# A state-space block with an FP4 FFN on one core: kept blocks in HBM, a lag of 20 steps, and the norms' squares on ScalarE

## The reference

```python
# first part, per sequence
x_proj, z = split(x @ W_in)                      # 256 -> 2 x 512
x_conv = silu(causal_conv4(x_proj) + conv_b)     # along the tokens
ssm = x_conv @ W_xproj                           # 33 columns: delta, B (16), C (16)
delta = softplus(ssm[..., 0])
h_mean = einsum(x_conv, delta * B) / L           # a sum over the WHOLE sequence
y = (h_mean x C + D * x_conv) * silu(z)
x = layernorm(x + y @ W_out)
# second part, per token: FP4 rounding in blocks of 16 before each product
h = silu(fp4(x) @ fp4(w_gate)) * (fp4(x) @ fp4(w_up))   # 256 -> 704
x = layernorm(x + fp4(h) @ fp4(w_down))
```

## Time and profile before

| | |
|---|---|
| three runs | 2200.66, 2203.39, 2206.25 us |
| the profiled execution | 2204.03 us, its span 2202.1 us |
| PE, PEld | 1990.6 us (90%), 1583.8 (72%) |
| DVE | 1756.7 us (80%) |
| ACT, POOL | 1111.5 (50%), 1115.6 (51%) |
| granted PE clock, mean | 0.98 |
| DMA | 90.53 MB, queue share 12.2% |
| chain that ended last | PE 76%, issue 5%, DVE 4%, ACT 3% |

### The profile page before, as it was taken

One profiled execution on the slowest core, in us unless ns is written; L12 is line 12 of the kernel. 1 busy time (PEld: TensorE's weight loads), 2 busy tenths in 40 slices (PEclk: granted clock), 3 DMA queues, 4 the chain that ended last, 5 costly groups with the idle time before them and its releaser, 6 DMA issues.

```text
span 2202.1 us, 37847 instructions
## 1 busy us (share of the span) xinstructions
PE 1990.6 (90%) x10532; PEld 1583.8 (72%) x10532; DVE 1756.7 (80%) x3548; ACT 1111.5 (50%) x2100; POOL 1115.6 (51%) x1643
## 2 busy tenths in 40 slices
PE   1887899899999999899999999899999999877776
PEld 1655688688877888688877888688876888666665
DVE  6234788798978888789877888798887888788875
ACT  2665455555545555455544556455544555423332
POOL 2223455466545556455644555465554556445543
PEclk9999999999999999999999999999999999999998
DMA  2111111111111111111111111111111111000000
GB/s 79 50 56 43 34 49 44 44 43 45 49 41 34 44 48 45 36 49 49 41 38 41 44 44 48 38 49 44 39 41 39 49 45 35 29 20 25 20 20 15
DMA packets 77089, 90.53 MB, mean 41 GB/s; under 512 B 8881, under 2 KB 59953, under 8 KB 76849
## 3 DMA queue, kind: packets, MB, share of 16 engines
q1 hardware_dynamic: 76848, 87.73, 12.2%
HBM read 37.37 MB, written 16.78 MB: 25 GB/s over the span
## 4 chain that ended last, share of the span: by engine, by line
PE 76%; issue 5%; DVE 4%; ACT 3%; POOL 1%; ACTq 0%; DVEq 0%; POOLq 0%
PE pgu L489 23%; PE pd L489 14%; PE pd L537 9%; PE pa L489 6%; PE pb L489 6%; PE pc L571 4%; PE pc L519 4%; PE pe_ L631 2%; PE pa L559 2%; PE pc L496 2%; PE pe_ L548 1%; PE pd L638 1%; DVE hbuf L990 1%; DVE qsh L820 1%; PE pa L615 1%
## 5 line engine op out<-in xcount | busy, mean ns | idle before, releaser
L489 PE MATMUL pgu<-wgu_hi,xqT 128*128 128x512 f32 (+1 forms) x1536 | 427.7, 387 | 0.9 <-issue 0.9
L489 PE MATMUL pd<-wd_hi,hqT 128*128 128x256 f32 (+1 forms) x1536 | 334.5, 299 | 18.7 <-DVE r L1012 15.5
L489 PEld LDWEIGHTS pgu<-wgu_hi,xqT 128*128 128x128 f32 x1536 | 279.8, 190 | 75.8 <-issue 27.6
L537 PE MATMUL pd<-wout,g 128*128 128x256 f32 x1024 | 259.9, 398 | 49.6 <-DVE hqT L980 35.2
L489 PEld LDWEIGHTS pd<-wd_hi,hqT 128*128 128x128 f32 (+1 forms) x1536 | 255.8, 190 | 57.4 <-issue 23.8
L946 DVE SCALAR_TENSOR_TENSOR acc<-xps,cw,acc 128x512 f32<-128x512 f32 x256 | 248.7, 972 | 24.4 <-POOL acc L429 23.7
L418 POOL TENSOR_SCALAR rs<-mv 128x1 f32<-128x1 f32 x128 | 61.6, 481 | 396.4 <-DVE mv L1027 228.8
L537 PEld LDWEIGHTS pd<-wout,g 128*128 128x128 f32 x1024 | 191.5, 195 | 79.7 <-issue 56.0
L741 ACT ACTIVATE hqT<-pe_ 128x512 fp32r<-128x512 f32 x128 | 76.2, 595 | 335.3 <-PE pe_ L631 335.3
L402 POOL TENSOR_TENSOR xv<-xnq,qsx 128x256 f32<-128x256 bf16 x128 | 79.5, 621 | 300.1 <-DVE xnq L839 300.1
L489 PE MATMUL pgu<-wgu_lo,xqT 128*128 128x512 f32 (+1 forms) x768 | 228.3, 379 | 0.0
(11 more groups left out here) (132 smaller groups left out, 4669.2 us busy)
## 6 DMA issues: line engine op xcount, KB each, us to landing
xcr<-xcs SPq DMA_DIRECT2D x128, 256.0 KB, 2.3
xin<-in_L_attn_x_dram SPq DMA_DIRECT2D x32, 512.0 KB, 3.9
xres<-in_L_attn_x_dram SPq DMA_DIRECT2D x128, 128.0 KB, 2.1
out_dram<-outb SPq DMA_DIRECT2D x128, 128.0 KB, 1.7
szr<-in_L_attn_W_in_dram SPq DMA_DIRECT2D x1, 1024.0 KB, 7.4
szr<-in_L_ffn_w_down_dram SPq DMA_DIRECT2D x1, 704.0 KB, 8.6
szr<-in_L_ffn_w_gate_dram SPq DMA_DIRECT2D x1, 640.0 KB, 4.5
szr<-in_L_ffn_w_up_dram SPq DMA_DIRECT2D x1, 640.0 KB, 5.7
```

Of the source, the lines that this page charges most:

```text
L489: mm = pe.matmul(bank, lhsT, rhs, start=(m == 0), stop=(m == len(pairs) - 1))
L537: mm = pe.matmul(pd[:, 0:DM], g[:, (s + 1) % 2, c, j * P:(j + 1) * P], wout[:, c, :], start=(c == 0), stop=(c == NB - 1))
```

## The change

- `szr` and `xcr` go. Silu(z) and the convolved block are written to two HBM tensors and read back into `xl` and `zl`, two slots each, one step ahead. The weights' scratch space moves.
- The second half runs 20 steps behind (`LAG` = 5 supersteps) instead of 16, so there is no late y; the state's division by L (`hcat`) stands at the end of the fourth step of the next sequence's first superstep. `walk` unrolls eight supersteps, then loops over sequences 2 to 7.
- The norms: DVE's two adds now also put out their sum (`accum_out`), ACT squares the deviations with an output of their sum (`deviations`), POOL works from these. The four statistics operations on DVE go.
- The order of every engine's step is written anew. The transposes of h put their last two blocks into `pb` instead of `pd`; the last norm's add comes at the start of the next step; C's transposes move from j = 1 to j = 3. h's two rounding steps stay the last DVE operations of their step, and h's product with the scales the last of POOL's.

```diff
+    LAG = SPS + 1
...
+    xc_hbm = nc.dram_tensor("xc_hbm", [NT, P, ST], F32)
+    sz_hbm = nc.dram_tensor("sz_hbm", [NT, P, ST], F32)
...
-        szr = sb("szr", [P, NB, SPS, ST])
-        xcr = sb("xcr", [P, NB, SPS, ST])
+        xl = sb("xl", [P, 2, ST])
+        zl = sb("zl", [P, 2, ST])
+        szs = sb("szs", [P, 2, ST])
...
+        def walk(body, fori, last=0):
+            for g in range(2 * SPS):
+                body(g, g % SPS, g // SPS)
+            with fori(2, B - last) as b:
...
+                    body(b * SPS + s, s, b)
+            for g in range(NSUP - last * SPS, NSUP + LAG + 2):
+                body(g, g % SPS, g // SPS)
...
+        def stages(g, j):
+            u = 4 * g + j
+            w = u - 4 * LAG
+            return u, u - 1, w, w - 4, w - 5, w - 6, w - 7, w - 8
+        def second(s):
+            return (s - LAG) % SPS
...
+                    if exists(w + 1):
+                        n, half = (j + 1) % 2, 16 * (2 * i + (j + 1) // 2 + 1)
+                        wait_apart(q, (xc_saved[n], half), (sz_saved[n], half), (g_ready, w))
+                        q.dma_start(xl[:, n, :], xc_hbm[w + 1]).then_inc(xl_landed[n], 16)
...
+                    if j == 1 and exists(g_, NSUP) and not (isinstance(g_, int) and g_ == NSUP - 1):
...
-                        jb, sb_ = ring_place(s, j)
-                        wait_apart(q, (xc_ready, v + 1), (yd_done, w))
-                        q.dma_start(xcr[:, jb, sb_, :], xcs[:, jb % 2, :]).then_inc(xc_saved[jb % 2], 16)
+                        q.wait_ge(xc_ready, v + 1)
+                        q.dma_start(xc_hbm[v], xcs[:, (j + 1) % 2, :]).then_inc(xc_saved[(j + 1) % 2], 16)
...
+                    if exists(u):
+                        q.wait_ge(z_ready, u + 1)
+                        q.dma_start(sz_hbm[u], szs[:, j % 2, :]).then_inc(sz_saved[j % 2], 16)
...
+            def layer_norm(n, ssq_done, taken, eps_done, rs_done, nm_done, total, ssq, rs, nm):
+                wait_apart(pool, (ssq_done, n + 1), (taken, n))
...
+                pool.tensor_tensor(rs[:, :], rs[:, :], nhalf[:, :], ALU.pow).then_inc(rs_done, 1)
...
+                    if p2:
+                        pool.wait_ge(yd_done, w + 1)
+                        pool.wait_ge(zl_landed[j % 2], 16 * (2 * i + j // 2 + 1))
+                        pool.tensor_tensor(g[:, second(s) % 2, j, :], g[:, second(s) % 2, j, :], zl[:, j % 2, :],
+                                           ALU.mult).then_inc(g_ready, 1)
...
+            def transposed_h(td, u):
+                pe.wait_ge(hprod_done, td + 1)
+                pe.wait_ge(z_ready, capped(u, NT))
+                for n in range(FC + 1):
+                    bank = pe_[:, n * P:(n + 1) * P] if n < 4 else pb[:, (n - 4) * P:(n - 3) * P]
...
+            def y_product(j, s, b, g_, v, w):
+                wait_apart(pe, (h_ready, b - 1 if s == 0 else b), (ct_ready, g_ - LAG + 1), (yd_done, w),
+                           (ssm_added, capped(v, NT)))
...
+            def state_projection(j, jb, g_, v, w):
+                pe.wait_ge(xc_ready, v + 1)
+                at_least(pe, yd_done, w + 1)
...
+            def z_product(j, u, td):
+                at_least(pe, z_ready, u)
+                at_least(pe, hqT_hi, 2 * td + 2)
+                at_least(pe, hqT_lo, 2 * td + 2)
...
+            def transposed_c(g_, v):
+                wait_apart(pe, (cc_ready, g_), (xct_copied, capped(v + 1, NT)))
...
+                    if exists(tg):
                         gate_and_up(tg)
+                    if p1:
+                        x_product(j, g_, u, v)
                     if exists(td):
...
+                        transposed_h(td, u)
+                    if p2:
+                        y_product(j, s, b, g_, v, w)
+                    if exists(to):
+                        output_projection(j, s, i, tz)
+                    if j == 1 and tail:
+                        partial_state(g_, w)
                     if j != 1 and exists(v):
...
+                        state_projection(j, jb, g_, v, w)
+                        transposed_conv(jb, u, v)
                     if exists(tx):
                         transposed_x(td, tx)
...
+                    if p1:
+                        z_product(j, u, td)
+                    if j == 1 and exists(v):
+                        state_projection(j, jb, g_, v, w)
+                        transposed_conv(jb, u, v)
+                    if j == 3 and tail:
+                        transposed_c(g_, v)
                     if exists(td):
                         down_projection(to, td)
...
+            def deviations(summed, n, r, total, ssq, ssq_done):
+                act.wait_ge(summed, n + 1)
+                act.activation(dev[:, :], r, ACT.Square, bias=total[:, :], scale=-1.0 * DM,
+                               accum_out=ssq[:, :]).then_inc(ssq_done, 1)
...
+                    if exists(tz):
+                        deviations(r2_done, tz, r2[:, :], sum2, ssq2, ssq2_done)
...
+                    if exists(v):
...
+                        act.activation(xcs[:, jb % 2, :], acc[:, :], ACT.Silu).then_inc(xc_ready, 1)
+                    if exists(tg):
+                        act.wait_ge(gu_pe, tg + 1)
+                        at_least(act, hq_link, 6 * tg)
+                        act.activation(hbuf[:, 0:FF], pgu[:, 0:FF], ACT.Silu).then_inc(sg_ready, 1)
+                    if p1:
+                        act.wait_ge(xp_pe, u + 1)
+                        at_least(act, conv, 2 * u)
+                        at_least(act, tap_done, u)
+                        act.activation(xps[:, KC - 1:KC - 1 + ST], pa[:, :], ACT.Copy)
+                        at_least(act, xc_ready, u)
+                        act.activation(acc[:, :], pa[:, :], ACT.Identity, bias=cb[:, j:j + 1],
+                                       scale=cw[:, j, KC - 1:KC]).then_inc(xp_copied, 1)
...
+                    if exists(to):
+                        deviations(r_done, to, r1[:, j, :], sum1, ssq1, ssq1_done)
...
+                    if exists(tz):
+                        dve.wait_ge(dn_pe, tz + 1)
+                        at_least(dve, out_ready, tz)
+                        dve.scalar_tensor_tensor(r2[:, :], pd[:, 0:DM], 1.0, r1[:, j, :], ALU.mult, ALU.add,
+                                                 accum_out=sum2[:, :]).then_inc(r2_done, 1)
...
-                    if p2 and not late_y(j, s):
-                        y_skip(i, j, s, w)
                     if exists(tx):
...
+                    tap(1)
                     tap(2)
                     if exists(tx):
...
+                    if exists(tg):
+                        dve.wait_ge(sg_ready, tg + 1)
+                        dve.tensor_tensor(h, h_big, pgu[:, FF:2 * FF], ALU.mult).then_inc(h_done, 1)
+                        dve.wait_ge(h_done, tg + 1)
+                        q_absmax(h, small_h).then_inc(hq_link, 1)
...
-                                          pd[:, 0:2 * P].rearrange("p (c n) -> p c n", c=2),
+                                          pb[:, 0:2 * P].rearrange("p (c n) -> p c n", c=2),
                                           hqT[:, 4:6, :], ALU.subtract).then_inc(hqT_lo, 1)
...
+                    if p2:
+                        dve.wait_ge(y_pe, w + 1)
+                        dve.wait_ge(xl_landed[j % 2], 16 * (2 * i + j // 2 + 1))
+                        at_least(dve, o_pe, 4 * i - 4)
+                        dve.scalar_tensor_tensor(g[:, second(s) % 2, j, :], xl[:, j % 2, :], dsk[:, j:j + 1], pc[:, :],
+                                                 ALU.mult, ALU.add).then_inc(yd_done, 1)
...
                     if exists(to):
                         dve.wait_ge(o_pe, to + 1)
...
+                        at_least(dve, r1_ready, to)
+                        dve.scalar_tensor_tensor(r1[:, j, :], pd[:, 0:DM], 1.0, xres[:, j % 2, :], ALU.mult, ALU.add,
+                                                 accum_out=sum1[:, :]).then_inc(r_done, 1)
                     if exists(tg):
                         dve.wait_ge(hq_link, 6 * tg + 3)
                         q_divide(h, small_h, h).then_inc(hq_link, 1)
...
                     if exists(tg):
                         dve.wait_ge(hbig_ready, tg + 1)
-                        q_add(h, hbuf[:, 0:FF]).then_inc(hq_link, 1)
+                        q_add(h, h_big).then_inc(hq_link, 1)
+                        at_least(dve, hprod_done, tg)
                         dve.wait_ge(hq_link, 6 * tg + 5)
-                        q_take(h, hbuf[:, 0:FF], hnq[:, :]).then_inc(hq_link, 1)
...
+                        q_take(h, h_big, hnq[:, :]).then_inc(hq_link, 1)
...
+                    if j == 3 and s == 0 and tail:
+                        dve.wait_ge(h_added, g_)
+                        dve.tensor_scalar(hcat[:, :], hacc[:, :], 1.0 / L, None, ALU.mult)\
```

(39 more changed lines are left out.)

529 lines of the change are left out of this document (179 added, 350 removed).

## The result

The changed kernel takes 2338.94 us (median of 4 runs, 2335.06 to 2339.92) against 2202.06 us (2200.66 to 2206.25) for the kernel before: ratio 1.0615, 95% interval 1.0595 to 1.0635. The forecast was 2229, with a range up to 2270. The direction was right, the size was 26 us instead of 137.

A forecast was written before the change was run, and what follows sets the result against it. The prediction took PE as the bound, then stalled by y's read. It summed start 55.2, first half 138, next two 85, full supersteps 1595, jumps and states 24, end 330 to 2227, forecast as 2229 us, range 2165 to 2270.

The forecast's parts named there:

- The wait of y's read: In every step PE waits 0.97 us ahead of the state projection, from 8.13 to 9.10, for DVE to read y.
- the sum: Steady superstep: 15.7 + 18.1 + 14.5 + 15.5 = 63.8 us against 60.0; the whole program 2229 us.
- So it fits, with 0.3 to spare: DVE's round: h's take 0.8 late, Silu of the gate ends at 5.3, before `xps` wants ScalarE at 5.63.
- The third rival: DVE's round is the bound, through POOL's holds and dearer adds with a sum: superstep 66.0, whole 2284, chance 0.13.
- States and jumps: At sequence boundaries: five loop jumps at 4 us each, state operations delaying the next step about 0.6, 24 us together.
- The two ends: The program before and after the full supersteps, forecast to cost 33 us more than in the kernel before.
- Start: First half alone: five supersteps of 27.6 us, 138 in all, with 0.5 a step saved as Silu(z) leaves the loop.
- next two: Two supersteps in which the second half and its FFN start: 85 us, from 95.2 with a late y of 10.
- last stretch: From the last full superstep to the end: 330 us, steps of 12.1 against 12.71, 0.6 less over 24 steps.
- POOL's hold of the h division: In j = 3, POOL's g multiplication may delay DVE's h division 0.8 to 0.9 us; PE's wait taken as 0.45.
- Norms on ScalarE: ACT's Square of 256 columns taken as 0.6 us, DVE's add with a summed output as 0.45.
- HBM-kept blocks: Four 256 KB transfers per step instead of one, costed at nothing, with 5 to 6 us of cover.

The follow-up runs named there:

- experiment 3: Changed kernel with ScalarE's copies xct (except j = 1) and xqT ahead of |h| instead of behind it: 2274.79 us, ratio 1.0330.
- experiment 1: Changed kernel with DVE's read of y ahead of the search for h's largest values and the hqT_lo subtractions: 2286.11 us, ratio 1.0378.
- experiment 4: Changed kernel with both y read ahead of h's search for largest values and xct and xqT copied ahead of |h|: 2186.09 us, ratio 0.9927.
- experiment 6: Changed kernel with the three operations on the sequence's state ahead of DVE's wait for xqT in j = 3: 2319.58 us, ratio 1.0533.
- experiment 12: Changed kernel with y read early, xct and xqT ahead of |h|, state operations earlier, spare matmuls in the last stretch: 2151.96 us, ratio 0.9773.
- experiment 7: Changed kernel with six unread 128x512 matmuls ahead of the down projection once the first half has ended: 2317.02 us, ratio 1.0524.
- experiment 8: Changed kernel with unread matmuls behind input transposes and ahead of state projections, in the first five supersteps alone: 2327.70 us, ratio 1.0571.
- experiment 9: Changed kernel with DVE's two conv taps ahead of the xt_lo subtractions while only the first half runs: 2334.88 us, ratio 1.0612.
- experiment 10: Changed kernel with C's transposes and their copy back in j = 1, in the first five supersteps alone: 2333.99 us, ratio 1.0599.

## Why the prediction was wrong

**The wait of y's read: right.** 0.97 us a step were forecast, 0.9 are there, at the place and with the releaser named. With xct and xqT out of the way (experiment 3) the superstep is 63.56, the sum said 63.8. There, counted from the start of gate and up, in j = 1 to 3 y's read ends at 9.1 (forecast 9.08) and PE's next product into pc starts at 9.2 (9.10). PE is done with the output projection at 8.5 instead of 8.13, so its wait is 0.68 in these steps and not 0.97: the forecast had the end of the wait right and its start 0.4 too early.

**"So it fits, with 0.3 to spare": the step that failed in the full supersteps.** DVE's round did not fit. The prediction had the take of h 0.8 late at the next gate and up, which is so (0.8 in j = 1, 0.9 in j = 3), but then Silu of the gate at 5.3, ahead of `xps` at 5.63. In the changed kernel's steady superstep Silu ends at 5.9 to 6.0 in three steps of four, y's read at 9.3 to 9.4, and C's transposes wait 0.74 for xct where 0.45 was taken. Two things were left out of the round. The copy of xqT behind |h| and xct, and xqT_lo behind it, stand between |h| and the rounding in every step, and experiment 3 shows what this order does: with both copies ahead of |h|, the takes of h that were late are done 0.1 ahead of the next gate and up or earlier, and Silu ends at 5.0 in j = 1 and j = 3. And POOL's product for h, started by the take, now runs beside DVE's x chain, so that the scale of x takes 0.88 instead of 0.17 in j = 1 and j = 3:

```profile
777.86 0.17 DVE L795 TENSOR_SCALAR qsx<-qsx 128x16 f32<-128x16 f32 x1
...
791.55 1.39 POOL L427 TENSOR_TENSOR hq<-hnq,qsh 128x704 f32<-128x704 bf16 x1 [2.82 <-DVE hnq L811]
792.09 0.88 DVE L795 TENSOR_SCALAR qsx<-qsx 128x16 f32<-128x16 f32 x1
```

With the h division at 1.27 instead of 0.88 in all four steps this is 3.0 us a superstep, and DVE's busy time is 12.9 a step, not the 12.1 of the forecast. Experiments 1, 3 and 4 show that the order is a limit of its own: without PE's waits for y the superstep is 64.65, and with the two copies moved as well 60.35, while y's read alone makes 63.56. In the steady superstep it costs only 1.2 us more than forecast (30 us over 25), but it makes DVE late everywhere. The third rival (DVE's round the bound, 66.0, 2284) had the place and, in POOL's holds, part of the reason; I gave it 0.13. That the order matters is shown by its removal. The holds are as long in experiment 4, where PE is the bound, so they alone don't bind; whether the order would bind without them no run shows.

**States and jumps: 24 forecast, 41 measured.** The state's three operations were put at 0.6 us; they cost 2.9 to 4.4 in the superstep behind them (experiment 6, 19 us for all). One of them runs beside POOL, 1.1 us longer for it, and DVE is late in these steps as it is. The jump's 4 us holds: supersteps s = 3 and s = 0 together are some 4 us above two steady ones.

**The two ends: 63 of the 111 us missed.** Start (138 against 162.5), next two (85 against 91.3), last stretch (12.1 a step against 13.6 on average). All three were made from durations of the kernel before with its clock. The changed kernel leaves PE waiting there, and its clock falls to 0.86 and 0.87. The 12.1 of experiment 12 does not bear the estimate out: that kernel has other orders and spare matmuls. With the clock up and nothing else changed (experiment 7) a step is 12.4 to 12.5, so of the 0.6 a step that the sum took off, 0.2 to 0.3 are there. Part of the stretch is the order too: experiments 1 and 3 each take 17 us off the time from the last superstep on. Experiments 7 and 8 show the clock's share: 22 us in the last stretch, 7 to 13 in the first five supersteps. What keeps the start at 149 instead of 138 with the clock up was not found; experiments 9 and 10 were tries at it.

**POOL's hold of the h division:** it takes 1.26 us on average over all 128 steps, where it takes 0.89 in the six steps in which POOL is still. The forecast had this hold in j = 3 alone, and at half its price. The x division stays at 0.43, unheld, though POOL's operations on 128x1 run beside most of them. The Trainium skill (SBUF — State Buffer, section "SBUF: two separate sides") says that VectorE with two SBUF inputs and GpSimd take a shared port pair as an exclusive lock; the trace agrees for POOL's products of 512 and 704 columns, with 0.89 to 1.27 here and 0.68 to 1.75 for hcat, and shows no hold by the 128x1 ones.

**Norms on ScalarE:** right. Square takes 0.51, and the accumulator read of 0.19 ends 0.61 behind its start, where 0.6 was taken. An add with a sum on DVE takes 0.36 to 0.42; its accumulator read of 0.08 runs beside its end, where 0.45 was taken for both. The Trainium skill (VectorE: DVE Perf Modes, section "Two Vector instructions with no wait between them") counts such an operation as two instructions; the trace shows the two, and the second adds nearly nothing.

**HBM-kept blocks:** costed at nothing, right for the steady superstep, at most 16 us in all.

## What to carry to other kernels

In an in-order queue, an operation moved behind one that waits for another engine inherits that wait for everything behind its own readers too; follow each moved result to its last reader on every engine, not only to the next wait of the bound engine. A new order also brings new neighbours: price an operation beside what another engine will run at that time. When two limits lie within a few per cent, test their removals together: the one alone gave a third, the other two fifths of what both gave. And where a change leaves TensorE waiting, take its durations from rows at the lower clock, or the ends of the program come out too short.

## What was not expected of the hardware

- Adding 138 matmuls made the kernel 22 us faster (experiment 7): in the last stretch PE was busy 82% of the time (297.64 of 363.00) and still ran at a granted 0.87.
- A small VectorE operation can be held for as long as a large one: the scale of x, 128x16, takes 0.17 us alone and 1.07 at most, median 0.72, in the changed kernel; all that took over 0.3 ran beside POOL's product for h.
- One operation on 16 partitions, 0.68 us alone, took 1.75 us beside POOL's product for h, seven times of eight.
